# Routing written into the attention block, and gathers of normed rows with an adding scatter, in a macaron layer on one core

## What is computed

```python
x = x + 0.5 * ffn(layernorm(x))      # 8 experts, 128 -> 512 -> 128
x = x + attn(layernorm(x))           # 16 heads of width 8, sequences of 1024
x = x + 0.5 * ffn(layernorm(x))

def ffn(x):
    indices = argmax(softmax(x @ Wr + br))        # one expert per token
    out = zeros_like(x)
    for i in range(8):
        xi = x * (indices == i)                   # the others enter as zero rows
        out += relu(xi @ W1[i] + b1[i]) @ W2[i] + b2[i]
    return out
```

## Time and profile before

| | |
|---|---|
| median of 3 runs | 1084.89 us (1082.17 to 1086.7) |
| the profiled execution's own time | 1084.15 us |
| its span, first to last instruction | 1082.3 us |
| TensorE / VectorE / ScalarE / GpSimd busy | 84% / 77% / 69% / 19% of the span |
| first route | 0 to 47.8 us |
| first mixture's items, to the reload | 47.8 to 169.9 us |
| attention, to its last exponential | 169.9 to 914.4 us |
| attention's end and second route | 916.4 to 958.2 us |
| second mixture's items | 958.2 to 1071.2 us, end at 1082.3 us |

### The profile page before, as it was taken

How to read it: one execution, slowest core, us unless ns; L and a number is a source line. 1 busy time by engine, 2 the same in 40 slices (tenths; PEclk the granted TensorE clock), 3 DMA queues, 4 the chain that set the end, 5 groups by cost and what they waited for, 6 DMA issues and landing times. The chain is left out here.

```text
span 1082.3 us, 17594 instructions
## 1 busy us (share of the span) xinstructions
PE 910.4 (84%) x5773; PEld 383.3 (35%) x5847; DVE 835.0 (77%) x1408; ACT 752.1 (69%) x1499; POOL 201.3 (19%) x295
## 2 busy tenths in 40 slices
PE   3635994779999999999999999999999997441896
PEld 2525993322222222222222222222222232331896
DVE  6822666979999999999999999999999955670564
ACT  4213772868888888888888888888888876320674
POOL 1172551464000001000000000001000000046254
PEclk9766997889999999999999999999999998665899
DMA  8436114782202203202202212022020000513011
GB/s 278 143 105 165 34 36 149 233 251 70 58 18 64 59 26 80 57 17 57 66 19 71 56 37 58 28 57 70 28 72 18 17 16 19 157 54 102 14 35 34
DMA packets 68473, 79.18 MB, mean 73 GB/s; under 512 B 13176, under 2 KB 45600, under 8 KB 68384
## 3 DMA queue, kind: packets, MB, share of 16 engines
q1 hardware_dynamic: 61744, 64.98, 21.6%
q0 software_dynamic: 5120, 12.59, 3.7%
q10 hardware_dynamic: 1520, 0.47, 0.2%
HBM read 40.60 MB, written 33.75 MB: 69 GB/s over the span
## 5 line engine op out<-in xcount | busy, mean ns | idle before, releaser
L1429 DVE TENSOR_REDUCE maxima<-ps_m 128x2 f32<-128x1024 f32 x512 | 602.8, 1220 | 59.0 <-PE ps_m L1244 54.8
L1410 ACT ACTIVATE probs<-ps_s 128x512 f32<-128x512 f32 x1024 | 555.4, 600 | 112.7 <-PE ps_s L1266 83.4
L1266 PE MATMUL ps_s<-q,k 74*128 74x512 bf16 (+1 forms) x950 | 296.0, 386 | 6.7 <-ACT probs L1410 4.3
L1277 PE MATMUL ps_o<-probs,vs 128*32 128x512 f32 x2048 | 273.6, 606 | 0.7 <-ACT probs L1410 0.7
L1266 PEld LDWEIGHTS ps_s<-q,k 74*128 74x128 bf16 (+1 forms) x1024 | 79.7, 97 | 309.4 <-ACT probs L1410 224.5
L1244 PE MATMUL ps_m<-k,q 64*128 64x512 bf16 x1024 | 159.9, 386 | 15.6 <-ACT probs L1410 7.9
L654 PE MATMUL ps_ha<-xsT,w1s 128*128 (+1 forms) x312 | 53.1, 296 | 59.7 <-ACT xsT L695 30.2
L695 ACT ACTIVATE xsT<-ps_x 128x128 f32<-128x128 f32 x64 | 17.7, 277 | 111.0 <-remote 54.6
L666 PE MATMUL ps_y<-W,hT 128*128 x624 | 88.1, 285 | 1.2 <-issue 0.6
L621 POOL DMA_INDIRECT v_and_ctx<-token_rows,source_i x64 | 62.1, 971 | 142.3 <-POOLq L331 123.4
L1244 PEld LDWEIGHTS ps_m<-k,q 64*128 64x128 bf16 x1024 | 49.0, 93 | 104.2 <-issue 59.1
(11 more groups left out here) (179 smaller groups left out, 547.9 us busy)
## 6 DMA issues: line engine op xcount, KB each, us to landing
k_rows<-parts SPq DMA_DIRECT2D x24, 384.0 KB, 4.3
sums<-oT SPq DMA_DIRECT2D x31, 256.0 KB, 3.9
q<-q_parts SPq DMA_DIRECT2D x75, 96.0 KB
k<-k_rows SPq DMA_DIRECT2D x15, 288.0 KB
token_rows<-x SPq DMA_DIRECT2D x16, 256.0 KB, 3.8
token_rows<-v_and_ctx SPq DMA_DIRECT2D x16, 256.0 KB, 3.8
k<-k_rows SPq DMA_DIRECT2D x15, 256.0 KB
q_parts<-parts SPq DMA_DIRECT2D x8, 384.0 KB, 3.4
```

Of the source, the lines that this page charges most:

```text
L1266: nc.tensor.matmul(ps_s[n % 3][:, :], k2[buffer(g)][0:contracted, j, kt * P:(kt + 1) * P], q2[buffer(g)][0:contracted, j, u * HALF:(u + 1) ...
L1277: last = nc.tensor.matmul(ps_o[32 * j:32 * (j + 1), :], vs[buffer(g)][:, kt, j, :], probs[:, s % 2, j, :], start=(kt == 0), stop=(kt == KT ...
L1410: nc.scalar.activation(probs[:, s % 2, j, :], ps_s[n % 3][:, :], ACT.Exp, scale=SCALE).then_inc(exped, 1)
L1429: nc.vector.tensor_reduce(maxima[:, :, pr, qt, kh], ps_m[slot][:, :, :], AX.X, ALU.max).then_inc(unit_free[slot], 1)
```

## The change

It has two parts. `Route` takes the place of `route`: the same work as methods, called inside the attention block. `Front` is the first mixture's norm and routing ahead of `Tiles`, without a barrier between; GpSimd itself waits for the stores and for `source_i`. The second mixture's routing stands at the end of the attention block on every engine, in attention's PSUM banks and in buffers that it no longer needs. The barrier ahead of the second `Tiles` stays.

Within routing: the steps up to the one-hot are done per half (`choose`); the counts come in the order of expert and tile and are scanned straight from PSUM; the place is formed with 2^23 added, so that its tile and row are bit fields; the `high_token` marks are made by ScalarE in 8 instructions; 64 matmuls of 32 columns add both parts in one accumulation, and one cast gives `source_i`. Half of the idle experts (32 of the 64 passes) come behind these matmuls on TensorE.

Then the table: `token_rows` is 128 wide and holds normed rows alone, so a gather moves 512 B per row where it moved 1 KB. The tokens are stored by SyncE to `x_rows` (or `out`) ahead of the items; the items add into a cleared tile `added`, and the scatter adds to DRAM (`compute_op=ALU.add`). VectorE clears each tile of `added` with a memset, 32 per mixture.

```diff
-                nc.vector.tensor_copy(count[:, :, :], ps_r[:, 1, :].rearrange("p (t e) -> p e t", e=EXPERTS)).then_inc(routed, 1)
...
-                nc.vector.tensor_scalar(tile_i[:, :], slot_f[:, :], 1.0 / P, None, ALU.mult).then_inc(routed, 1)
-                dve.wait_ge(routed, 17)
-                nc.vector.tensor_copy(rounded[:, :], tile_i[:, :]).then_inc(routed, 1)
...
-                nc.vector.tensor_tensor(marks[:, :, 0, :], hot[:, :, :],
-                                        w["high_token"][:, :].unsqueeze(2).to_broadcast([P, TILES, TILES]), ALU.mult)
+class Route:
...
+    def find(self, pe):
+        for t in range(TILES):
+            if t % QUAD == 0:
+                pe.wait_ge(self.marked, QUAD + t // QUAD + 1)
+                pe.wait_ge(self.column, t // QUAD + 1)
+            for a in range(2):
+                last = self.nc.tensor.matmul(self.ps_f[:, 0:TILES], self.columns[:, t, :], self.marks[:, t, a, :],
+                                             start=(t == 0 and a == 0), stop=(t == TILES - 1 and a == 1))
+        last.then_inc(self.f_full, 1)
...
+    def mark(self, act):
+        act.wait_ge(self.routed, self.FOUND - 1)
+        for i in range(QUAD):
+            self.nc.scalar.activation(self.marks[:, i::QUAD, 1, :], self.hot[:, i::QUAD, :], ACT.Copy, scale=self.w["low_token"][:, i:i + 1]).then_inc(self.marked, 1)
+        for q in range(QUADS):
+            tiles = slice(q * QUAD, (q + 1) * QUAD)
+            self.nc.scalar.activation(self.marks[:, tiles, 0, :], self.hot[:, tiles, :], ACT.Copy, scale=self.w["high_token"][:, q:q + 1]).then_inc(self.marked, 1)
...
+    def choose(self, dve, h):
+        tiles = slice(h * half, (h + 1) * half)
...
+    def arrange(self, dve):
...
+        dve.wait_ge(self.r_full, 1)
+        nc.vector.tensor_tensor_scan(self.upto[:, :, :].rearrange("p e t -> p (e t)"), self.ps_r[:, many - 1:2 * many - 1],
+                                     w["seg"][:, :, :].rearrange("p e t -> p (e t)"), 0.0, ALU.add, ALU.mult).then_inc(routed, 1)
...
+        bits = self.slot[:, :].bitcast(I32)
+        nc.vector.tensor_scalar(self.tile_i[:, :], bits, 7, TILES - 1, ALU.logical_shift_right, ALU.bitwise_and).then_inc(routed, 1)
+        nc.vector.tensor_scalar(self.row_i[:, :], bits, P - 1, None, ALU.bitwise_and).then_inc(routed, 1)
...
+        nc.vector.tensor_copy(self.routes.source_i[:, :], self.ps_f[:, 0:TILES]).then_inc(routed, 1)
+class Front:
...
+    def tensor(self, pe):
...
+        self.route.count(pe)
+        self.setup.tensor_idle(pe)
+        self.route.find(pe)
+        self.setup.tensor_idle_experts(range(self.setup.EARLY, EXPERTS))
...
+    def gpsimd(self, pool):
+        self.setup.gpsimd_masks(pool)
+        pool.wait_ge(self.route.stored, 2 * 16 * QUADS)
+        pool.wait_ge(self.route.routed, Route.FOUND)
@@ class Tiles @@
-                                         self.xs[:, t, D:], None, bounds_check=TOKENS - 1, oob_is_err=False).then_inc(self.y_stored[t % LEAVING], 16)
+                                         self.added[:, t, :], None, compute_op=ALU.add).then_inc(self.y_stored[t % LEAVING], 16)
...
+            dve.wait_ge(self.masked, self.MASKED + min(i, TILES - 1) + 1)
...
+        def clear(t):
+
+            nc.vector.memset(self.added[:, t, :], 0.0).then_inc(self.masked, 1)
@@ attention, sync @@
+                sp.wait_ge(vstep_2, 1)
+                for q in range(MERGED):
+                    route.store(sp, q, dram["results"], w["x"])
+                for q in range(MERGED):
+                    quad_normed(sp, q)
+                    route.store(sp, q, dram["token_rows"], xn_next)
@@ attention, tensor @@
-                for unit in FINISH:
+                for q in range(QUAD):
+                    turn_next(q)
+                slot, used = slot_of(("y", MERGED))
+                pe.wait_ge(unit_free[slot], used)
+                output(slot, MERGED, range(QUAD // 2))
+                route.logits(pe, 0)
+                output(slot, MERGED, range(QUAD // 2, QUAD)).then_inc(unit_full[slot], 1)
+                turn_next(QUAD)
+                route.turn_logits(pe, 0)
+                for q in range(QUAD + 1, QUADS):
+                    turn_next(q)
@@ kernel @@
-    dram["token_rows"] = nc.dram_tensor("token_rows", [TOKENS, 2 * D], F32).ap()
+    dram["token_rows"] = nc.dram_tensor("token_rows", [TOKENS, D], F32).ap()
```

More of the change, by code:

```diff
@@ L211, in tensor_idle, with tensor_idle_experts @@
         pe.wait_ge(self.dve_step, 2)
-        for e in range(EXPERTS):
+        self.tensor_idle_experts(range(self.EARLY))
+    def tensor_idle_experts(self, experts):
+        for e in experts:
             for c in range(HC):
@@ L269, in __init__ @@
         self.total, self.start, self.end = (sb(name, [P, EXPERTS], F32) for name in ("total", "start", "end"))
-def route(nc, w, dram, tag, xn_sb, routes, setup=None, ready=0):
-    x_sb = w["x"]
-    source_i, total, start, end = routes.source_i, routes.total, routes.start, routes.end
-    with ExitStack() as sub:
+class Route:
+    FOUND = 25
+    CHOSEN = 6
+    UNIT = float(2 ** 23)
+    def __init__(self, nc, memory, semaphores, w, dram, tag, xn_sb, routes, ps_t, ps_lT, ps_l, ps_r, ps_f, xnT, columns, marks):
@@ new lines, in sem2 @@
+            return semaphores.enter_context(nc.semaphore(name + tag))
+        self.nc, self.w, self.dram, self.xn_sb, self.routes = nc, w, dram, xn_sb, routes
+        self.ps_t, self.ps_lT, self.ps_l, self.ps_r, self.ps_f = ps_t, ps_lT, ps_l, ps_r, ps_f
+        self.xnT, self.columns, self.marks = xnT, columns, marks
+        self.logitT = sb2("logitT", [P, 2, QUAD * P], F32)
+        self.logit, self.first, self.ranked = (sb2(name, [P, TILES, EXPERTS], F32) for name in ("logit", "first", "ranked"))
@@ new lines, in turn, with logits @@
+    def turn(self, pe, q):
+        if q >= 2:
+            pe.wait_ge(self.t_out, q - 1)
+        for i in range(QUAD):
+            last = self.nc.tensor.transpose(self.ps_t[q % 2][:, i * P:(i + 1) * P], self.xn_sb[:, QUAD * q + i, :], self.w["ident"][:, :])
+        last.then_inc(self.t_full, 1)
+    def logits(self, pe, h):
+        pe.wait_ge(self.t_out, QUAD * (h + 1))
+        wait_unless_zero(pe, self.lT_out, h)
+        for j in range(QUAD):
+            last = self.nc.tensor.matmul(self.ps_lT[32 * j:32 * (j + 1), :], self.w["Wr"][:, :], self.xnT[:, QUAD * h + j, :], start=True, stop=True)
+        last.then_inc(self.lT_full, 1)
@@ L844, in vector @@
         self.mask_items(dve)
+        for t in range(2):
+            clear(t)
         dve.wait_ge(self.listed, self.LISTED)
@@ L1329, in _ @@
                 values(SOFT - 1)
-                for unit in FINISH:
-                    do_unit(*unit)
+                for q in range(QUAD):
[9 more added lines that the diff above has]
+                    turn_next(q)
+                pe.wait_ge(unit_free[free], freed + 1)
+                route.logits(pe, 1)
+                route.turn_logits(pe, 1)
+                route.count(pe)
+                route.find(pe)
             @block.scalar
```

547 lines of the change are left out of this document (269 added, 278 removed).

## The result

The changed kernel takes 1077.64 us (median of 7, 1076.13 to 1080.21) against 1084.89 us before: a ratio of 0.9946, 95% interval 0.9934 to 0.9959. Its profiled execution took 1078.64 us, with a span of 1076.8 us. Each comparison is made within its set; why there are two levels is the main thing the experiments looked for.

A forecast was written before the change was run, and what follows sets the result against it. The first gather's start was taken to set each mixture's end. From 1084.15 us, less 3.4 (first mixture), less 6.5 (second), plus 2.0 (landing) is 1076.25 us; forecast 1076 us, its own range 1071 to 1082, whole range 1035 to 1100.

The forecast's parts named there:

- Shared routing: Routing steps that both mixtures share, from the one-hot through the counts to the columns and last steps: 3.1 us less.
- One-hot: In routing, five VectorE passes go from 256 to 128 elements, 0.42 to 0.29 us: 0.65 us less in all.
- Marks: In routing, eight half-size marks on ScalarE at 0.43 us each, narrowly covered by the columns' 5.29 us.
- First mixture: Start of the first mixture's gathers: shared routing's 3.1 us and a barrier's 0.33 us, 3.4 us less in all.
- Second mixture: Second route at attention's end: 3.4 us less from the branch and turned quads, with the shared 3.1 us: 6.5 us.
- the stores: Attention's end: SyncE's token stores ahead of the transfer VectorE's divisions wait for, none to 1.48 us, taken as 0.3 us.
- the logits: Attention's end: first half's logits ahead of TensorE's second output half make that about 0.8 us late, VectorE's norm covering it.
- Gathers at nothing: GpSimd's gathers cost by rows, not bytes, so half the bytes gain nothing, nor does the wait behind them.
- The scatter's issue: Late in each mixture, GpSimd's adding scatter stays below 1.59 us, so the pace does not change; cost nothing.
- Its landing: Adding scatter's landing, at the reload behind the first mixture and the kernel's end: 1.0 us each, 2.0 us more.
- The wait behind the gathers: Items flow only once gathers are issued; rival that it belongs to their bytes: 1018 us gone, 1047 us halved, chance 0.15.
- the rival of the adding scatter as the bound: GpSimd's adding scatters at 2.26 us per item, 0.37 us over the pace, 23 us more, so 1099 us; chance 0.20.

The follow-up runs named there:

- experiment 4: Changed kernel with the one-hot table written by expert and tile, so the counts' matmuls read it in order; 1038.99 us where the kernel before took 1018.29 us.
- experiment 3: Kernel before with only the 512 B gathers and adding scatters, routing as before; 1046.35 us, ratio 1.0278, where the kernel before took 1018.29 us.
- experiment 8: Changed kernel with TensorE making the second half of attention's last output before the first half's logits; 1040.29 us, against 1037.87 us for the changed kernel.
- experiments 1 and 2: Changed kernel with overwriting scatters, 1013.12 us; kernel before with only the new routing, 1 KB gathers and plain scatters, 1014.00 us; kernel before 1018.29 us.
- free sets: Sets of runs in which the kernel before takes 1018 us.
- held set: A set of runs in which the kernel before takes 1083.9 to 1085.4 us, as in the first comparison.
- the same probe: Changed kernel with 140 small VectorE memsets ahead of item 0 in each mixture, 100 waiting for nothing; 1094.00 us, ratio 1.0089.

## Why the prediction was right, and where it was not

The forecast was 1076 us in a range of 1035 to 1100; it is 1077.64. Against the profiled execution's own 1084.15 us the sum said 7.9 us less and the trace has 5.5 us less. By the steps:

- **Shared routing, 3.1 us.** Counts to columns: 2.67 us gained, predicted 2.3. One-hot, predicted 0.65 us: the passes did gain it (from the logits to the end of the one-hot 1.91 us, before 2.57), and the counts took it back. Their matmuls read every eighth value and take 0.61 and 0.63 us instead of 0.28 to 0.31, which I had not priced, and VectorE waits 1.16 us for them, before 0.53; experiment 4 shows that the stride is the cause. Marks: the eight halves take 2.43 us, 0.30 us each against the 0.43 us I assumed, well under the columns' cover.
- **First mixture, 3.4 us.** 3.06 us at the first gather. At the last addition 1.94 us of it are left (1.1 us went while the items got going behind the gathers, which no run explains) and at the last scatter 0.37 us. The second half of the idle experts delayed nothing: the first tile starts at 47.86 us, 2.93 us before.
- **Second mixture, 6.5 us.** The gather moved by 5.21 us, of which 0.14 us had been lost by the reload: 5.35 us. At VectorE's wait for the den transfer, near attention's end, the kernel is 1.24 us behind the one before (923.17 against 921.93), 1.1 us of it lost in attention, and counted from there the step is 6.45 us. How long attention takes differs by more than that from run to run: from the end of the last scatter to the second mixture's first gather it is 789.7 us in the kernel before and 789.6 us in experiment 3, and between 783.1 and 787.4 us in twelve traces of kernels with the new routing. Of the 0.3 us for the stores and the 0.8 us for the logits nothing can be told from this; experiment 8 shows that the logits' place costs the addition 0.4 us and that moving them costs more. One number I gave was inconsistent with my own sum: 951.7 us for the second first gather left out the first mixture's 3.4 us and the reload's 1.0 us. With them it is 949.3 us, and 952.99 us was measured: nearly all of the first mixture's gain was gone by then. From the gather on the items got going 1.6 us sooner than before, unexplained too, and the last addition is 6.8 us earlier.
- **Gathers at nothing.** Right: 0.95 us at either width, and the kernels of experiments 1 and 2 agree.
- **The scatter's issue, below 1.59 us.** This is the step that failed, though the number was nearly right. It is 1.55 to 1.63 us, and I had compared it with the mean item of 1.89 us and so put its cost at nothing. Eight of the last nine items take 1.79 us, since they bring no tile to turn, and the last 1.2 us, so there the point from which it decides is at most 1.49 us. VectorE's last addition of the second mixture ends at 1068.23 us and the last scatter starts at 1069.76 us, 1.53 us behind it, before 0.80 us:

```profile
1067.82 0.41 DVE L847 SCALAR_TENSOR_TENSOR v_and_ctx<-y_sum,half_mask,v_and_ctx 128x128 f32 x1 [0.17 <-DVE y_sum L841]
```

With the 0.57 us that it takes longer itself, the second mixture loses 1.30 us; the first, by the same count, 1.57 us. That is 2.9 us for a term put at nothing.
- **Its landing, 1.0 us twice.** From the end of the last scatter to SyncE's reload it is 1.91 us, before 1.40: 0.5 us. At the kernel's end it is 5.49 us, before 5.47: nothing. So the landing, put at 2.0 us, was 0.5 us, and the issue, put at nothing, 2.9 us. The two misses, 1.5 us too much and 2.9 us too little, partly cancel, so that the forecast is off by 1.6 us only: this is in part luck. The Trainium skill, page DMA: Bandwidth & Descriptors, "Rules for kernel authors", has an accumulating DMA read its destination first; the 0.5 us and the longer issue fit, the end of the kernel does not show it.
- **The wait behind the gathers.** Correctly not priced for bytes: half the bytes, the same 45 us. But I took it for a property of the kernel. In the free sets the same kernel before does without it and takes 66 us less, where I had put the wait's worth at 58 us. There the first gather still sets the changed kernel's end, but through GpSimd's queue, and the rival of the adding scatter as the bound comes true. I gave it 0.20 with 1099 us; it comes to 2% more than the kernel before, for another reason than the 0.37 us per item that I worked out.

The range of 1035 to 1100 us would have taken in the 1037.87 us of the free set too; the direction would not have held there. "Faster" came true because the first comparison was made in a held set, where most of the adding scatters hide behind items that are late anyway, and that was luck as well. The part that makes this kernel faster at either level is the routing alone: 0.9953 (0.9939 to 0.9968) in a free set and 0.9932 (0.9915 to 0.9948) in a held one.

## What to carry to other kernels

A stretch in which every engine is idle for no releaser that the profile can name is not a constant of the kernel: before resting a sum on it, compare it over several sets of runs, and ask what would bound the kernel if it went. When an instruction in a queue of its own gets longer, count the queue from its first instruction to its last (here 32 gathers and 32 scatters) and not only against the mean pace of the items that feed it. Before a table is laid out anew, price the stride for every engine that reads or writes it: here it cost TensorE's read and VectorE's write, but not VectorE's read, and moving it from the one to the other gained 0.16 us and 0.04 us.

## What the runs showed of the hardware

- An indirect scatter of 128 rows of 512 B takes GpSimd 0.98 us, and 1.55 to 1.63 us if it adds. An indirect gather takes 0.95 us for rows of 512 B and of 1 KB.
- In held sets, while GpSimd issues gathers back to back, VectorE gets instructions through singly, 24 in 30.2 us, at steps of 0.7 or 1.4 us, after 15 that pass freely. It goes on for 5 us behind the last gather. Adding scatters back to back don't do this. TensorE and ScalarE are nearly idle in the same stretch (busy 2.91 and 0.51 of 30.7 us; ScalarE waits 30.42 us for a tile that TensorE has turned). One chip was free in one set and held in another; what decides it was not found, nor was the same probe made on the other engines.
- A matmul of 256 columns in bf16 takes 0.28 us if the moving operand lies in order (0.39 us at a granted clock of 0.50) and 0.61 us with a stride of eight values, at either clock; VectorE's write of 128 values in bf16 takes 0.29 us in order and 0.71 us with a stride of 32 values.
- Items whose engines read values from SBUF into registers slow from 1.90 us to between 2.57 and 3.65 us beside fills of about 200 GB/s; with constants in their place they do not.
